# Cross-attention with image-prompt tokens on one core: the stretch up to the loop rewritten, with the U products as tasks of the loop

## What is computed

```python
q = heads(hidden_states @ W_q)
k_t, v_t = heads(text_ehs @ W_k), heads(text_ehs @ W_v)
probs_t = softmax(einsum('bhsd,bhtd->bhst', q, k_t) * attn_scale)
text_out = einsum('bhst,bhtd->bhsd', probs_t, v_t)
k_ip, v_ip = heads(ip_ehs @ W_k_ip), heads(ip_ehs @ W_v_ip)
attn_scores = einsum('bhsd,bhnd->bhsn', q, k_ip) * attn_scale
qsem = l2norm(einsum('bhst,bte->bhse', probs_t, text_ehs))
sem = einsum('bhse,bne->bhsn', qsem, l2norm(ip_ehs))
probs_ip = softmax(attn_scores + SEM_SCALE * sem) * spatial_mask
out = (text_out + einsum('bhsn,bhnd->bhsd', probs_ip, v_ip)) @ W_out + b_out + hidden_states
```

## Time and profile before

| What | Value |
|---|---|
| median of 3 runs | 318.04 us |
| the profiled execution's own time | 319.01 us |
| its span, first to last instruction | 317.3 us |
| PE busy | 301.7 us, 95% of the span |
| ACT busy | 276.9 us, 87% |
| DVE busy | 269.5 us, 85% |
| POOL busy | 210.1 us, 66% |
| the span's first slices of 7.9 us, PE in tenths | 4, 8, 9, 9, 8 |

### The profile page before, as it was taken

How to read it: one execution, slowest core, us unless ns; L and a number is a source line. 1 busy time by engine, 2 the same in 40 slices (tenths; PEclk the granted TensorE clock), 3 DMA queues, 4 the chain that set the end, 5 groups by cost and what they waited for, 6 DMA issues and landing times.

```text
span 317.3 us, 8813 instructions
## 1 busy us (share of the span) xinstructions
PE 301.7 (95%) x2289; PEld 291.1 (92%) x2289; DVE 269.5 (85%) x1861; ACT 276.9 (87%) x1168; POOL 210.1 (66%) x372
## 2 busy tenths in 40 slices
PE   4899899999999999999999999999999999998976
PEld 3789769888999999999999999999999999998964
DVE  5483846798889898989898989998999899898995
ACT  3744679999999999999999999999999999999942
POOL 3033416687877789688977796889787878675200
PEclk9999999999999999999999999999999999999999
DMA  6980003000120202011110112021202120010011
GB/s 193 347 253 1 0 8 91 2 1 3 32 64 21 66 30 66 25 44 45 30 63 9 56 32 65 22 64 34 64 24 63 34 62 24 23 33 22 24 42 64
DMA packets 15130, 17.02 MB, mean 54 GB/s; under 512 B 2592, under 2 KB 14536, under 8 KB 15080
## 3 DMA queue, kind: packets, MB, share of 16 engines
q1 hardware_dynamic: 15080, 16.44, 17.1%
HBM read 10.55 MB, written 5.24 MB: 50 GB/s over the span
## 4 chain that ended last, share of the span: by engine, by line
PE 79%; DVE 8%; ACT 7%; DMA 2%; POOL 1%; issue 1%; SPq 1%; POOLq 0%
PE gv_ps L1073 23%; PE mi_ps L1108 12%; PE mi_ps L1032 12%; PE sc_ps L1052 10%; PE et_ps L1060 10%; ACT e_sb L619 4%; PE mi_ps L1086 3%; DMA x_nat<-in_x 2%; PE mi_ps L1010 2%; DVE place_ctxT L795 2%; PE gv_ps L1187 2%; PE mi_ps L1012 1%; DVE ktok L847 1%; PE sc_ps L1167 1%; DVE negmax L787 1%
## 5 line engine op out<-in xcount | busy, mean ns | idle before, releaser
L619 ACT ACTIVATE e_sb<-sc_ps,negmax 128x60 f32<-128x60 f32 x640 | 152.6, 353 | 6.3 <-DVE negmax L787 5.1
L795 DVE CUSTOM_DVE_ANT_0 place_ctxT<-gv_ps,e_sb 128x60 f32<-128x60 f32 x640 | 100.8, 213 | 16.9 <-PE gv_ps L1073 15.4
L1073 PE MATMUL gv_ps<-tab,place_w 128*128 128x160 f32 x640 | 113.1, 299 | 0.0
L1073 PEld LDWEIGHTS gv_ps<-tab,place_w 128*128 128x128 f32 x640 | 93.7, 189 | 0.3 <-ACT place_w L637 0.3
L1052 PE MATMUL sc_ps<-km,qs 128*128 128x256 f32 x320 | 77.0, 322 | 0.1
L637 ACT COPY place_w<-et_ps 128x256 f32<-128x256 f32 x160 | 68.5, 428 | 0.2
L1060 PE MATMUL et_ps<-ident,e_sb 128*128 128x128 f32 x320 | 61.9, 275 | 2.9 <-ACT e_sb L619 1.8
L787 DVE TENSOR_REDUCE negmax<-sc_ps 128x4 f32<-128x240 f32 x160 | 63.4, 397 | 0.0
L795 DVE DVE_READ_ACCUMULATOR2_ANT quad<- 128x1 f32 x640 | 52.5, 82 | 0.0
L420 POOL TENSOR_TENSOR km<-ktok,group_mask 128x512 fp32r<-128x512 f32 x40 | 41.3, 1039 | 14.4 <-DVE ktok L847 7.9
L628 ACT COPY fin<-gv_ps 128x80 f32<-128x80 f32 x160 | 43.8, 274 | 6.7 <-DVE quad L795 5.7
(11 more groups left out here) (184 smaller groups left out, 557.2 us busy)
## 6 DMA issues: line engine op xcount, KB each, us to landing
x_nat<-in_x SPq DMA_DIRECT2D x16, 320.0 KB, 3.2
out<-place_w SPq DMA_DIRECT2D x32, 160.0 KB, 1.8
place_ctx<-in_ctx SPq DMA_DIRECT2D x4, 256.0 KB, 3.3
place_w<-in_L_xattn_W_v SPq DMA_DIRECT2D x1, 640.0 KB, 8.0
place_w<-in_L_xattn_W_k SPq DMA_DIRECT2D x1, 640.0 KB, 9.4
place_w<-in_L_xattn_W_k_ip SPq DMA_DIRECT2D x1, 640.0 KB, 11.0
place_w<-in_L_xattn_W_v_ip SPq DMA_DIRECT2D x1, 640.0 KB, 9.5
place_ctxT<-in_L_xattn_W_out SPq DMA_DIRECT2D x1, 640.0 KB
```

The source lines that it names most:

```text
L619: last = nc.scalar.activation(e_sb[:, slot, TOK * j:TOK * j + T], sc_ps[:, bank, TOK * j:TOK * j + T], ACT.Exp, bias=negmax[:, slot, j:j + 1])
L795: last = v.tensor_tensor_reduce(out=junk[:, u % 2, j, 0:T], in0=gv_ps[:, u % 2, TABW * j:TABW * j + T], in1=e_sb[:, u % ERING, TOK * j:TOK ...
L1073: last = mm(gv_ps[:, u % 2, 2 * TABW * r:2 * TABW * r + 2 * TABW], eT[:, u % TRING, P * r:P * r + P], tab[:, b % 2, h:h + 2, :].rearrange( ...
```

## The change

1. ctx: one copy `ctxT` by DVE (all four pieces); ACT copies each piece to `ctx_hi` straight from PSUM when DVE has read it. `ctxM` is gone: `ip_dif` is taken first, then the normalised ip columns are written over those of `ctxT`, and G multiplies `ctxT` with itself.
2. PE runs 17 transposes of the identity into an unused bank (`idle_products`): 9 before the first context piece, then 3, 2, 2, 1 behind the pieces.
3. `ip_nat` is loaded by ACT's queue; W_k_ip is loaded behind W_q; the 64-row copy of W_out and the bias are loaded once G and `ctx_lo` are made.
4. V of the first three pairs goes by parts: high by high of all three, then low by high, then high by low. 
5. Scores 0 and 1 stand before K's third part; V_ip stands behind V of the last pair; on ACT W_out's high part stands behind the V copies, on DVE each low part of K is followed by a low part of q, and the low part of `wo_parts` is made by POOL.
6. The five U products become tasks of units 1, 2, 4, 6 and 9 in the banks of `mi_ps`, copied by DVE; placing starts after the third; the first batch's `u_all` is made at unit 14 instead of 12.

```diff
+        U_AT, U_PARTS = (1, 2, 4, 6, 9), (0, 2, 4, 1, 3)
+        for n, at in enumerate(U_AT):
+            MISC[at] = ("u", n, 0)
...
             return {"x": (xT_lo, 2 * index + n + 1), "q": q_copied_at(n, index) if by_pool else q_lo_at(n, index), "v": (v_copied, PAIRS),
+                    "u": (u_copied, n + 1),
...
-            return b if s == 12 and b < B else None
+            return b if s == (12 if b else 14) and b < B else None
...
-                if q == 0:
-                    sp.dma_start(ip_nat[:], ctx_tokens[:, T:TOK, :]).then_inc(in_ip, DMA)
...
-            sp.dma_start(wkip, w_k_ip.rearrange("(c p) n -> p c n", p=P)).then_inc(in_wkip, DMA)
...
             load_square(wq_nat, w_q, in_wq, (0, 64))
+            sp.dma_start(wkip, w_k_ip.rearrange("(c p) n -> p c n", p=P)).then_inc(in_wkip, DMA)
...
-            sp.wait_ge(u_copied, 5)
-            place_u(0)
+            sp.wait_ge(ctx_lo_made, 1)
+            sp.wait_ge(pre_g, 1)
             sp.dma_start(u_nat[0:64], w_out[2 * P:C, :].unsqueeze(1).to_broadcast([64, B, C])).then_inc(u_shared, DMA)
...
+            sp.wait_ge(u_copied, 3)
+            place_u(0)
+            sp.wait_ge(u_copied, 5)
...
+            pool.wait_ge(wo_hi_made, 1)
+            g.tensor_tensor(wo_parts[:, 1], wo[:, 0:2], wo_parts[:, 0].bitcast(F32), ALU.subtract).then_inc(wo_lo_made, 1)
...
+            act.dma_start(ip_nat[:], ctx_tokens[:, T:TOK, :]).then_inc(in_ip, DMA)
             nc.scalar.preload_act_table_set("natural_log_exp_and_others")
...
-                if q % 2 == 0:
-                    act.wait_ge(pre_ctxT, q + 1)
-                    nc.scalar.copy(ctxT[:, :, P * q:P * q + P],
...
-                nc.scalar.copy(ctxM[:, :, P * q:P * q + P].rearrange("p c (b t) -> p c b t", t=TOK)[:, :, :, 0:T],
...
+                act.wait_ge(ctxT_made, q + 1)
+                nc.scalar.copy(ctx_hi[:, :, P * q:P * q + P],
+                               BANKS[q].rearrange("p (c t) -> p c t", c=EC)).then_inc(ctx_hi_made, 1)
             x_hi(0, 0)
             x_hi(0, 1)
-            act.wait_ge(ctxT_act, 2)
-            act.wait_ge(ctxT_dve, 2)
-            nc.scalar.copy(ctx_hi, ctxT).then_inc(ctx_hi_made, 1)
...
-            for n in range(5):
-                rows = 96 + B * (n % 2 == 0)
-                act.wait_ge(pre_u, n + 1)
-                nc.scalar.copy(u_sb[0:rows, n], BANKS[U_BANKS[n]][0:rows, 0:C]).then_inc(u_copied, 1)
...
+            def copy_u(n):
+
+                part = U_PARTS[n]
+                rows = 96 + B * (part % 2 == 0)
+                dve.wait_ge(pre_u, n + 1)
+                v.tensor_copy(u_sb[0:rows, part], mi_ps[0:rows, misc_bank(("u", n, 0)), 0:C]).then_inc(u_copied, 1)
+
+            k_low(0)
+            q_low(0, 0)
+            k_low(1)
+            q_low(0, 1)
             maxima(0)
-            q_low(0, 1)
             maxima(1)
+            k_low(2)
             q_low(0, 2)
...
+            def idle_products(n):
+
+                for _ in range(n):
+                    tr(BANKS[4][:, 0:P], ident[:], ident[:])
+
             pe.wait_ge(ident_made, 1)
+            idle_products(9)
...
+            for part in range(3):
+                if part == 1:
+                    pe.wait_ge(ctx_lo_made, 1)
+                if part == 2:
+                    pe.wait_ge(wv_lo_made, 1)
+                for q in range(PAIRS - 1):
+                    v_steps(q, BANKS[q], part)
...
+            def u_product(n):
+
+                m, part = divmod(U_PARTS[n], 2)
+                if n == 0:
+                    pe.wait_ge(vip_made, QC)
+                    pe.wait_ge(in_wo, 2 * DMA)
+                pe.wait_ge(*bank_released(("u", n, 0)))
...
+            k_product(0)
+            pe.wait_ge(wq_lo_made, 1)
+            q_project(0, 0)
+            pe.wait_ge(g_copied, 2)
+            k_product(1)
+            q_project(0, 1)
+            pe.wait_ge(v_copied, 2)
             scores(0)
             scores(1)
+            k_product(2)
+            pe.wait_ge(wq_pair_made, 2)
+            q_project(0, 2)
             pe.wait_ge(q_lo, 2)
+            for part in range(3):
+                v_steps(PAIRS - 1, mi_ps[:, 1, :], part)
+            vip_product()
             x_transposes(1, 0)
             x_transposes(1, 1)
```

More of the change, by code:

```diff
@@ L123, in xattn_kernel @@
         neg_half = sb("neg_half", [P, HEADS])
-        ctxT, ctxM = (
-            place_ctxT[:, EC * B * TOK * n:EC * B * TOK * (n + 1)].rearrange("p (c t) -> p c t", c=EC) for n in range(2))
+        ctxT = place_ctxT[:, 0:EC * B * TOK].rearrange("p (c t) -> p c t", c=EC)
         ipn = sb("ipn", [B * NIP, E])
@@ L468, in builds @@
                 if k == 0 and b == 0:
+                    pool.wait_ge(pre_v, PAIRS)
+                if k == 7 and b == 0:
                     pool.wait_ge(v_copied, PAIRS)
@@ L659, in _ @@
             nc.scalar.copy(wq_hi[:], wq_nat).then_inc(wq_hi_made, 1)
-            act.wait_ge(in_wo, 2 * DMA)
-            nc.scalar.copy(wo_parts[:, 0], wo[:, 0:2]).then_inc(wo_hi_made, 1)
             for q in range(PAIRS - 1):
@@ L664, in _, with k_high @@
                 nc.scalar.copy(v_sb[:, q, :], BANKS[q][:, 0:C]).then_inc(v_copied, 1)
-            for m in range(QC):
+            def k_high(m):
                 act.wait_ge(pre_k, m + 1)
@@ L671, in _ @@
                                              BANKS[K_BANKS[m]][64 * a:64 * a + 64, :], ACT.Copy, scale=SCALE).then_inc(k_hi, 1)
-                if m > 0:
-                    q_high(0, m - 1)
+            act.wait_ge(in_wo, 2 * DMA)
+            nc.scalar.copy(wo_parts[:, 0], wo[:, 0:2]).then_inc(wo_hi_made, 1)
+            k_high(0)
+            q_high(0, 0)
+            k_high(1)
+            q_high(0, 1)
+            k_high(2)
             q_high(0, 2)
@@ L806, in _ @@
             v.tensor_scalar(ip_ssc[:], ip_ss[:], EPS * EPS, None, ALU.max).then_inc(ip_step, 1)
[L807 removed]
+            for q in range(PAIRS):
                 dve.wait_ge(pre_ctxT, q + 1)
[L809 removed]
+                v.tensor_copy(ctxT[:, :, P * q:P * q + P], BANKS[q].rearrange("p (c t) -> p c t", c=EC)).then_inc(ctxT_made, 1)
                 if q == 1:
@@ L1153, in _, with v_steps @@
             last.then_inc(pre_g, 1)
+            pe.wait_ge(ctx_hi_made, PAIRS)
             pe.wait_ge(wv_hi_made, 1)
-            def v_product(q, bank):
+            def v_steps(q, bank, part):
                 tokens = slice(P * q, P * q + P)
-                steps = [(cc[:, c, tokens], ww[:, c, :]) for cc, ww in ((ctx_hi, wv_hi), (ctx_lo, wv_hi), (ctx_hi, wv_lo))
-                         for c in range(EC)]
-                for n, (cc, ww) in enumerate(steps):
-                    if q == 0 and n == EC:
-                        pe.wait_ge(ctx_lo_made, 1)
-                    if q == 0 and n == 2 * EC:
-                        pe.wait_ge(wv_lo_made, 1)
-                    last = mm(bank[:, 0:C], cc, ww, start=n == 0, stop=n == len(steps) - 1)
-                last.then_inc(pre_v, 1)
@@ L1170, in _ @@
-            for q in range(PAIRS - 1):
-                v_product(q, BANKS[q])
-            pe.wait_ge(wk_lo_made, 1)
-            pe.wait_ge(ip_dif_made, 1)
-            pe.wait_ge(in_wkip, DMA)
-            text_hi, text_lo = (cc.rearrange("p c (b t) -> p c b t", t=TOK)[:, :, :, 0:T] for cc in (ctx_hi, ctx_lo[:]))
-            for m in range(QC):
-                if m == 1:
-                    pe.wait_ge(g_copied, 2)
-                if m == 2:
-                    pe.wait_ge(v_copied, PAIRS - 1)
+                cc, ww = ((ctx_hi, wv_hi), (ctx_lo, wv_hi), (ctx_hi, wv_lo))[part]
@@ new lines, in v_steps @@
+                for c in range(EC):
+                    last = mm(bank[:, 0:C], cc[:, c, tokens], ww[:, c, :], start=part == c == 0, stop=part == 2 and c == EC - 1)
+                if part == 2:
+                    last.then_inc(pre_v, 1)
+            for part in range(3):
+                if part == 1:
+                    pe.wait_ge(ctx_lo_made, 1)
+                if part == 2:
+                    pe.wait_ge(wv_lo_made, 1)
+                for q in range(PAIRS - 1):
+                    v_steps(q, BANKS[q], part)
@@ L1211, in _ @@
             pe.wait_ge(zeros_made, 6)
+            pe.wait_ge(v_copied, 3)
             e_transposes(0)
-            pe.wait_ge(vip_made, QC)
-            pe.wait_ge(in_wo, 2 * DMA)
+            scores(2)
             pe.wait_ge(k_lo, 2 * GROUPS)
-            for n in range(5):
-                m, part = (n // 2, n % 2) if n < 4 else (2, 0)
-                if n > 2:
-                    pe.wait_ge(u_copied, n - 2)
-                rows = 96 + B * (part == 0)
-                first = 0 if part == 0 else 96 + B
-                mm(BANKS[U_BANKS[n]][0:rows, 0:C], vip_bd[0:QROWS[m], m, first:first + rows], wo[0:QROWS[m], m, :],
-                   start=True, stop=True).then_inc(pre_u, 1)
-                if n == 2:
-                    scores(2)
-            pe.wait_ge(u_copied, 5)
             e_transposes(1)
```

96 lines of the change are left out of this document (48 added, 48 removed).

## The result

| | before | after |
|---|---|---|
| median (16 runs each, side by side) | 318.64 us (317.13 to 320.0) | 316.92 us (313.92 to 317.66) |
| profiled execution: time / span | 319.01 / 317.3 us | 317.4 / 315.6 us |
| its mean granted clock of PE | 1.000 | 0.989 |

The ratio is 0.9921 (95% interval 0.9899 to 0.9942): 2.5 us faster by it, 1.7 by the medians, where 4.5 us were forecast (313.5 us, range 311.8 to 316.3). Of the 3.4 us between 313.5 and 316.92, 0.6 are the base: three runs of the kernel before gave 318.04, sixteen give 318.64. All ratios leave out runs of over 1.5% above the fastest of their kernel, which are four of experiment 10, one of experiment 5 and one beside it.

What follows compares the result with a forecast made beforehand. PE was taken as the bound mid-program, which the change leaves alone; 6.0 us saved before the loop minus 1.5 us lost in the first ten units gave 4.5 us, so 318.04 became 313.5 us, range 311.8 to 316.3.

Steps and rivals of the forecast that it cites:

- Part 2: From V's end to the loop: loop begins at 40.7 us instead of 46.66, 6.0 us saved, 2.6 of them here.
- Then PE runs out of work first, and DVE closes the stretch: Before the loop: PE finishes x transposes at 37.8 us; V_ip's spreading, x's low parts, maxima and ACT's exponentials last until 40.65.
- The forecast's own doubt about the clock: At G, before V: a fast PE ends V at 18.3 us, a clock falling again before x at 20.4.
- The 6.0 us: Start up to the loop: total saving, 3.4 us from V and 2.6 after it; bounds 4.5 and 6.7.
- Part 1: Up to V's end: V ends at 19.0 us instead of 22.37, gaining 3.4 us (2.0 to 4.1).
- My scaling by 0.60 to 1.11: At G: its 4.64 us shrink to about 2.7 us, as x's four transposes took 0.60 at fast pace against 1.11.
- the U products and the waits around them: Between V's end and the loop: source of 2.6 us of the saving.
- Part 3: First ten units: U products make PE the bound, and the units take 1.5 us longer (0.8 to 2.7).
- slower: First ten units: two banks of `mi_ps` chain DVE into PE's order, 7.7 us lost, 319.7 us; chance 0.06.
- the 0.46 us at the end of the units: End of the first ten units: PE's idleness that ACT's exponentials ended; winning it back gave the lower bound, 0.8 us.
- U in full: First ten units: U's 2.7 us come on top of ACT's unchanged delays, saving 3.3 us, 314.7 us; chance 0.14.
- start not faster: Before K: PE slow through G or W_k_ip landing at 20.4 us or later, 3.1 us saved, 314.9 us; chance 0.13.

Runs made afterwards that it cites:

- experiment 10: Changed kernel plus idle transposes before the loop and near the end, with scores 0 and 1 and DVE's low parts in the old order: 321.77 us.
- experiment 5: Changed kernel plus 18 identity transposes in PE's pause near the end, none before the loop: ratio 0.9902 to the kernel before.
- experiment 1: Also called fill_entry: changed kernel plus 18 identity transposes in PE's pause right before the loop: 314.62 us, ratio 0.9881.
- experiment 4: Kernel before plus identity transposes near the end and eight in the pause ahead of q's third part: 318.12 us, ratio 0.9957.
- experiment 8: Changed kernel plus idle transposes before the loop and near the end, without the 17 identity transposes at the start: 314.68 us.
- experiment 6: Changed kernel plus idle transposes near the end only, with U products back ahead of the loop, copied by ACT: 314.73 us, ratio 0.9865.
- experiment 7: Changed kernel plus idle transposes before the loop and near the end, with each U product made twice: 317.25 us, ratio 0.9948.
- experiment 3: Kernel before plus 18 identity transposes in PE's pause near the end: 318.06 us, ratio 0.9986.
- reorder_bare: Changed kernel with exponential transposes 0 and 1 and scores 2 and 3 ahead of x transposes and V_ip, no fillers: 313.83 us, ratio 0.9833.

## Why the prediction was wrong

**The step that failed** is in Part 2: "Then PE runs out of work first, and DVE closes the stretch". It gave a pause of PE from 37.8 to 40.7 us, and the sum took it as a delay only, with every product behind it at its usual duration. The pause was 2.19 us long, and in the profiled execution PE's granted clock fell to 1.2 GHz behind it and again behind the one near the end. That is 1.6 us in the ten units (experiment 1) and 1.1 at the end (the account), 2.7 us together. In 12 of 16 executions the mean clock is below 1.000, in eight of them at the 0.989 of the profiled one. The forecast's own doubt about the clock stood at the wrong place: it was asked of G at 10 us, where PE turned out fast, and not of the pause at 38 us. That the column read 1.00 in the profiled execution of before, the pause near the end included, was taken as if it would do so after.

**A second term was measured on an unusual execution.** The 6.0 us were counted from the profiled execution of before, where K began at 22.37 us (22.22 in PE's timeline). In the trace of experiment 4 the same stretch of code let it begin at 20.64. Taking 0.97 us off the time for the median did not take the late start off the gain. This fits with the change being worth 3.0 to 3.8 us at an unbroken clock (experiment 4) and not 4.5.

**Part 1** was right in its result, 19.0, with some luck: terms under it were off and cancelled. x's transposes started at 8.47, not 9.4, and G took 3.84 us, not 2.7. My scaling by 0.60 to 1.11 took all of the 4.64 us before as slow; but the 18 transposes of experiment 1 (2.12 us, 0.118 each) show that G's 32 instructions (3.84, 0.120 each) were at the full pace now, so that only a part of it had been slow before. The path was another one too: G waited for DVE's `place_ctxT` until 9.86, not for x, and V stood behind G on PE; `ctx_lo` was ready at 13.41, just before. ACT's copies from PSUM left the path, as said. W_k_ip was no matter: K began when V ended. That the identity transposes keep PE fast is not shown (experiment 8): of four traces without them two are as fast. POOL's subtraction in `wo_parts` took 1.55 us, not 1.2, and delayed nothing on the path.

**Part 2** was right in time: the loop began at 40.30, said was 40.7, and by the steps that were named: in DVE's timeline the spreading of V_ip ran from 36.43 to 37.54, directly ahead of x's low parts, the maxima and ACT's exponentials. PE's own sum left out the first exponential transposes and scores 2 and 3, which filled the start of the pause. The prediction put the whole 2.6 us of this part on "the U products and the waits around them". By PE's timelines K's start to the loop's took 24.44 us before, 23.45 with the new order and U ahead (experiment 6), and 21.48 after: about 1.0 us is the order of K, q and V_ip, mostly the 0.96 us wait ahead of q's third part, and 1.97 are the U products. These 1.97 are paid back in the units, so of the 2.96 us the 1.0 stays.

**Part 3** was right in kind and a little small. PE is the bound of the ten units (experiment 7), and five U products lengthen them by 16.53 - 14.57 = 1.96 us at full clock, where 1.5 was taken and 0.8 to 2.7 were the bounds. PE's own work was as forecast, 15.8 us. The rest are waits in units 4 and 9, which take 1.91 and 1.84 us in the trace of experiment 1 where the other U units take 1.54: 0.7 us together, where 0.3 was allowed. In unit 9 the U product waited 0.22 us for DVE's `xl`, the copy that frees its bank, which is the mechanism of the rival that ended slower, at one task. In unit 4 the table products' weights waited for ACT's copy of the transposed exponentials. That the 0.46 us at the end of the units are won back was right.

**The rivals.** U in full (314.7) and start not faster (314.9) did not happen; slower did not either. The measured 316.92 came from a term that no rival had. By the profiled executions the sum holds nearly once the clock's 2.7 us are put aside: 6.4 - 1.96 = 4.4 us against 4.5 forecast. But this holds only against that execution of before; by the runs it is 3.0 to 3.8. The four executions of the changed kernel at clock 1.000 took 313.9 to 315.0 us.

The Trainium skill ("TensorE: Matmul & The Clock Gate", Part 1), cited in the prediction for the start alone, bears on every pause: it says that TensorE goes back to 1.2 GHz when it has been idle. The windows of after agree in the direction: 0.50 behind a pause of 2.19 us. The Trainium skill ties the fall to a longer idle time than this one, or than the 0.96 us of experiment 3; here the measurements decide. That it happens in some executions and not in others, with the pauses in both, is what the runs add.

**Open:** why the same pause near the end lets the clock fall in some executions and not in others: in about half of those of the kernel before (31 of the 64 runs beside these experiments are at 0.995 or less), in one of six of fill_entry and in three of five of reorder_bare at most. And what makes some executions start late at the same granted clock, which moves the times of both kernels by 1 us and more.

## What to carry to other kernels

Where PE bounds a kernel, a new pause of PE of about 2 us is to be costed with what stands behind it at half pace, here 1.1 to 2.3 us in most executions and up to 5.4 in experiment 10 (323.31 against 317.9 us), and not only as its own length. A gain read off one profiled execution is to be checked against a second one: here the start of the kernel before moved by 1.6 us between two. First move the chain that closes the stretch (maxima and exponentials) ahead of PE work that nobody waits for; if that can't be done, fill the pause with transposes that write to an unused bank. And before moving products from the entry into a loop, see who bounds the loop's first units: if it is PE, as here, the move wins nothing (experiment 6).

## What the runs showed of the hardware

- Behind a pause of about 2 us the granted clock falls to 0.50 in some executions and not in others: the mean is below 1.000 in 12 of 16 of the changed kernel, and the profiled one of before keeps 1.00 behind 2.17 us. One of 0.96 us was followed by a fall too (experiment 3), and the stretch at 0.50 was longer there, some 7 us.
- The granted clock column does not show the slow start. In before, x's transposes took 1.11 us for four with the column at 1.00, about what four take at 0.50 (1.05 us at 42.80 in the trace of experiment 3).
- One execution of experiment 5 took 616.57 us and one of the kernel before beside it 644.36 us, both with a mean granted clock of 1.0. The former is the profiled one. Its column reads 1.00 in the windows between 6 and 100 us, where PE is as slow as at the end, at 608 us. From its timeline:

```profile
105.30 0.72 PE L1079 MATMUL et_ps<-ident,e_sb 128*128 128x128 f32 x2
```

  That is 0.72 us where the earlier trace rows has 0.38. So a column that reads 1.00 is no proof of pace; the durations of a known instruction are.
- The issue of `ip_nat`'s load took 1.29 us on ACT's queue, in after's timeline of ACT, where it had taken 0.88 on SP's. It delayed nothing here.
